# Splitting the shared weights w13 once in the up stages, storing both parts, and grouping rank-2 products by twos

## What is computed

```python
# first: I = 2752; of |silu| the lower-ranked half of each row is set to 0
s = silu(x @ w_gate.T); s[k = I/2 smallest |s| per row] = 0
x1 = layernorm(x + (s * (x @ w_up.T)) @ w_down.T)
# second: weights tiled four times along the input, and rank-2 terms
lin(x, wq, A, B) = x @ tile(wq, (1, 4)).T + 0.5 * (x @ A.T @ B.T)
out = layernorm(x1 + lin(silu(lin(x1, w1q, a1, b1)) * lin(x1, w3q, a3, b3), w2q, a2, b2))
```

## Time and profile before

| | us |
|---|---|
| median of 3 runs | 1863.69 (1860.75 to 1864.17) |
| the profiled execution | 1862.13 |
| its span | 1860.2 |
| TensorE busy (products) | 1840.7 |
| VectorE, ScalarE, GpSimd busy | 1468.3, 719.9, 957.5 |
| DMA, mean over the span | 139 GB/s |

### The profile page before, as it was taken

How to read it: one execution, slowest core, us unless ns; L and a number is a source line. 1 busy time by engine, 2 the same in 40 slices (tenths; PEclk the granted TensorE clock), 3 DMA queues, 4 the chain that set the end, 5 groups by cost and what they waited for, 6 DMA issues and landing times.

```text
span 1860.2 us, 23661 instructions
## 1 busy us (share of the span) xinstructions
PE 1840.7 (99%) x8584; PEld 1533.3 (82%) x8584; DVE 1468.3 (79%) x2077; ACT 719.9 (39%) x1177; POOL 957.5 (51%) x705
## 2 busy tenths in 40 slices
PE   9999999999999999999999999999999999999998
PEld 8898888978889789888888988888887777777776
DVE  2138899988988695898878768988588899889973
ACT  4346544474233434722343365233323232223312
POOL 5446697546655854465466545554568232023410
PEclk9999999999999999999999999999999999999999
DMA  4333248734377743334786334366953112312212
GB/s 147 93 101 97 86 147 236 204 98 142 97 232 227 226 129 104 113 128 131 236 256 195 93 107 142 98 212 193 278 179 141 35 46 101 135 62 77 102 46 91
DMA packets 123511, 258.65 MB, mean 139 GB/s; under 512 B 13860, under 2 KB 35876, under 8 KB 120168
## 3 DMA queue, kind: packets, MB, share of 16 engines
q1 hardware_dynamic: 118784, 240.34, 41.7%
q10 hardware_dynamic: 4608, 16.78, 2.2%
HBM read 215.65 MB, written 41.42 MB: 138 GB/s over the span
## 4 chain that ended last, share of the span: by engine, by line
PE 83%; POOL 5%; DVE 5%; ACT 4%; DMA 3%; issue 1%; SPq 0%; POOLq 0%; DVEq 0%; ACTq 0%
PE banks L1596 28%; PE banks L1597 27%; PE banks L1598 27%; POOL wl L659 3%; ACT junka L815 2%; DMA w_in_place<-in_wg 2%; DVE junkx L1083 1%; PE banks L1788 1%; POOL xTl L659 1%; ACT wh L766 1%; POOL w2l L659 1%; DMA w_in_place<-in_wd 0%; DVE qa L1125 0%; POOL w L688 0%; PE banks L1801 0%
## 5 line engine op out<-in xcount | busy, mean ns | idle before, releaser
L659 POOL TENSOR_TENSOR wl<-w_in_place,wh 128x512 fp32r<-128x512 f32 (+2 forms) x552 | 751.8, 1367 | 573.1 <-ACT wh L766 571.9
L766 ACT CAST wh<-w_in_place 128x512 fp32r<-128x512 f32 (+2 forms) x560 | 329.0, 589 | 724.2 <-DMA w_in_place<-in_wg 281.2
L1596 PE MATMUL banks<-wh,xTh 128*128 128x512 f32 (+2 forms) x1536 | 565.0, 368 | 5.4 <-POOL wl L659 5.3
L1598 PE MATMUL banks<-wh,xTl 128*128 128x512 f32 (+2 forms) x1536 | 563.2, 367 | 0.0
L1597 PE MATMUL banks<-wl,xTh 128*128 128x512 f32 (+2 forms) x1536 | 563.1, 367 | 0.0
L1596 PEld LDWEIGHTS banks<-wh,xTh 128*128 128x128 f32 x1536 | 288.3, 188 | 51.4 <-POOL wl L659 9.6
L1598 PEld LDWEIGHTS banks<-wh,xTl 128*128 128x128 f32 x1536 | 288.3, 188 | 40.1
L1597 PEld LDWEIGHTS banks<-wl,xTh 128*128 128x128 f32 x1536 | 288.3, 188 | 39.6
L1596 PE MATMUL banks<-wh,hTh 128*128 128x512 f32 x672 | 263.2, 392 | 2.2 <-POOL wl L659 2.1
L1598 PE MATMUL banks<-wh,hTl 128*128 128x512 f32 x672 | 262.2, 390 | 0.0
L1597 PE MATMUL banks<-wl,hTh 128*128 128x512 f32 x672 | 262.2, 390 | 0.0
(11 more groups left out here) (151 smaller groups left out, 2194.9 us busy)
## 6 DMA issues: line engine op xcount, KB each, us to landing
w_in_place<-in_wd SPq DMA_DIRECT2D x176, 256.0 KB, 2.7
w_in_place<-in_wg SPq DMA_DIRECT2D x128, 256.0 KB, 3.0
w_in_place<-in_wu SPq DMA_DIRECT2D x128, 256.0 KB, 2.7
turning<-squares SPq DMA_DIRECT2D x16, 1024.0 KB, 5.1
landed<-turning SPq DMA_DIRECT2D x64, 256.0 KB, 3.9
w_in_place<-in_w SPq DMA_DIRECT2D x54, 256.0 KB, 2.9
x_in_place<-in_xT SPq DMA_DIRECT2D x32, 256.0 KB, 5.2
y<-in_xtok SPq DMA_DIRECT2D x4, 2048.0 KB, 8.5
```

Source lines behind the costliest of these rows:

```text
L659: nc.gpsimd.tensor_tensor(lo, landed, hi.bitcast(F32), ALU.subtract).then_inc(done, 1)
L766: nc.scalar.copy(hi, piece).then_inc(hi_done, 1)
L1596: nc.tensor.matmul(dst, ah, bh, start=start, stop=False)
L1598: return nc.tensor.matmul(dst, al, bh, start=False, stop=stop)
```

## The change

- In up of block b = 1 to 3, w13 is split piece by piece, a piece being one of the 22 (pair, w) tiles of 128 x 512. Piece q is loaded by SyncE at i = 14 + 4k (k the count within the block, at most 8), cast by ScalarE and subtracted by GpSimd behind their own work of i + 2, and both parts are stored to a new DRAM tensor `split13` by SyncE at i + 4, where SyncE waits for `w13_lo`. Blocks 1 and 2 take eight pieces (i = 14 to 42), block 3 six (to 34). The buffers are the places of `xt`.
- In both halves `load_13` loads both parts, four transfers of 256 KB a pair; `high_13` and `low_13` are gone. The first two pairs are loaded at d = 40 and 42 of the last down. `w13h` and `acc` change places.
- In pairs 1 to 10, bb = 1 issues its rank-2 products first, right behind those of bb = 0, with both `s_done` and `h_done` waited for in front of them; its dense products follow, the last one of each w signalling.

```diff
+SPLIT_AT, SPLITS = 14, 8
+def splits(b):
+    return [(q, SPLIT_AT + 4 * (q - SPLITS * (b - 1))) for q in range(2 * PAIRS) if q // SPLITS == b - 1]
...
+                        for q, at_piece in splits(b):
+                            if i == at_piece:
+                                load_split(b, q)
+                        for q, at_piece in splits(b):
+                            if i == at_piece + 4:
+                                keep_split(q)
                     if b < NB - 1 and i >= NG - 3:
                         load_x(b + 1, i - (NG - 3))
+            def load_split(b, q):
+                if q % SPLITS == 0:
+                    sp.wait_ge(u_freed, 8 + 4 * NJ * b + 1)
+                    sp.sem_inc(passed_sp, 1)
+                if q >= 2:
+                    sp.wait_ge(w13_out, 32 * (q - 1))
+                sp.sem_inc(passed_sp, 1)
+                sp.dma_start(raw13[q % 2][:, :], w13[q // 2, q % 2, :, :]).then_inc(raw13_in[q % 2], 16)
+            def keep_split(q):
+                sp.wait_ge(w13_lo, q + 1)
+                sp.sem_inc(passed_sp, 1)
+                sp.dma_start(split13[q // 2, q % 2, 0], hi13[q % 2][:, :].bitcast(F32)).then_inc(w13_out, 16)
+                sp.dma_start(split13[q // 2, q % 2, 1], lo13[q % 2][:, :].bitcast(F32)).then_inc(w13_out, 16)
...
             def load_13(h, p):
                 n = PAIRS * h + p
                 if n >= 2:
-                    sp.wait_ge(w13_used, n - 1)
+                    sp.wait_ge(uu_done, 4 * (n - 1))
...
-                    sp.dma_start(w13_in_place[:, n % 2, w, :], w13[p, w, :, :]).then_inc(w13_in[n % 2][w], 16)
+                    sp.dma_start(w13h[:, n % 2, w, :].bitcast(F32), split13[p, w, 0]).then_inc(w13_in[n % 2][w], 16)
+                    sp.dma_start(w13l[:, n % 2, w, :].bitcast(F32), split13[p, w, 1]).then_inc(w13_in[n % 2][w], 16)
...
+            def low_split(q):
+                pool.wait_ge(w13_hi, q + 1)
+                less(hi13[q % 2][:, :], lo13[q % 2][:, :], raw13[q % 2][:, :], w13_lo)
...
+            def high_split(q):
+                act.wait_ge(raw13_in[q % 2], 16 * (q // 2 + 1))
+                nc.scalar.copy(hi13[q % 2][:, :], raw13[q % 2][:, :]).then_inc(w13_hi, 1)
...
+            def low_rank_terms(h, p, bb, first):
+                s, rows = number(h, p, bb), rows_of(p // 2)
+                for i in range(2):
...
+                    for w, done in enumerate((gg_done, uu_done)):
+                        p0 = QUAD[2 * i + w]
+                        ins = nc.tensor.matmul(banks[4 * (s % 2) + 2 * w + i][0:rows, :], b13[p0:p0 + 3 * R, mm],
+                                               lx[p0:p0 + 3 * R, bb, :], start=first, stop=not first)
+                        if not first:
+                            ins.then_inc(done, 1)
...
+                first = p > 0 and bb == 1
+                if first:
+                    pe.wait_ge(s_done, s - 1)
+                    pe.wait_ge(h_done, s - 1)
+                    pe.sem_inc(passed_pe, 1)
+                    low_rank_terms(h, p, bb, True)
...
                     if bb == 0:
-                        pe.wait_ge(w13_lo, 2 * n + w + 1)
+                        pe.wait_ge(w13_in[n % 2][w], 32 * (n // 2 + 1))
...
-                                        k == 0, False)
+                                        k == 0 and not first, first and k == KQ - 1)
+                        if first:
+                            ins.then_inc((gg_done, uu_done)[w], 1)
...
+                if not first:
+                    low_rank_terms(h, p, bb, False)
```

More of the change, by code:

```diff
@@ L93 @@
 FOLDS = 2 * CQ
+SPLIT_AT, SPLITS = 14, 8
+assert SPLIT_AT + 4 * SPLITS < NG and (NB - 1) * SPLITS >= 2 * PAIRS
 SENT_0 = (16, 20, 24, 32, 36, 43)
@@ L204, in program @@
     folded = nc.dram_tensor("folded", (3, P, NT * HQ), F32, kind="Internal").ap()
+    split13 = nc.dram_tensor("split13", (PAIRS, 2, 2, P, 512), F32, kind="Internal").ap()
     turning = nc.dram_tensor("turning", (NB, NJ, P, NT * CW), F32, kind="Internal").ap()
@@ L279, in program @@
         assert at["scr"] + 5 * H <= at["mags"]
+        places = (at["scr"], at["junkd"])
+        hi13 = [sb(f"hi13{i}", [P, 512], F32R, 4, offset=o) for i, o in enumerate(places)]
+        lo13 = [sb(f"lo13{i}", [P, 512], F32R, 4, offset=o + 2048) for i, o in enumerate(places)]
+        raw13 = [sb(f"raw13{i}", [P, 512], F32, 4, offset=o + 2048) for i, o in enumerate(places)]
         over = {"at": at["v"]}
@@ L308, in program @@
         lx = put("lx", [P, 2, TB], F32R)
-        acc = put("acc", [P, 2, R, TB], F32)
+        w13h = put("w13h", [P, 2, 2, 512], F32R)
         assert over["at"] <= at["y"]
@@ L318, in program @@
         hq1l = put("hq1l", [P, CQ, TB], F32R)
-        w13h = put("w13h", [P, 2, 2, 512], F32R)
+        acc = put("acc", [P, 2, R, TB], F32)
         assert over["at"] <= at["sgn"]
@@ L323, in program @@
         fold = (sb("fold0", [P, CQ, TB], F32, 4, offset=at["hq0l"]), sb("fold1", [P, CQ, TB], F32, 4, offset=at["hq1l"]))
-        w13_in_place = sb("w13_in_place", [P, 2, 2, 512], F32, 4, offset=at["w13l"])
         ya = (sb("ya0", [P, 2, H], F32, 4, offset=at["w13l"]), sb("ya1", [P, 2, H], F32, 4, offset=at["w13h"]))
@@ L377, in program @@
             sem("small_in"), sem("b_zero"), sem("b_in"), sem("b_ready"), sem("sel_ready"))
-        w13_hi, w13_lo, w13_used = sem("w13_hi"), sem("w13_lo"), sem("w13_used")
+        raw13_in, w13_out = [sem(f"raw13_in{i}") for i in range(2)], sem("w13_out")
+        w13_hi, w13_lo = sem("w13_hi"), sem("w13_lo")
         l_ready = sem("l_ready")
@@ L470, in load_tokens @@
                 sp.wait_ge(x1_out, 16 * NT * (b + 1))
+                if t == 0:
+                    sp.sem_inc(passed_sp, 1)
+                    sp.wait_ge(w13_out, 32 * min(SPLITS * (b + 1), 2 * PAIRS))
                 if n >= 2:
@@ L583, in load_13 @@
                     sp.sem_inc(passed_sp, 1)
-                    sp.dma_start(w13_in_place[:, n % 2, w, :], w13[p, w, :, :]).then_inc(w13_in[n % 2][w], 16)
+                    sp.dma_start(w13h[:, n % 2, w, :].bitcast(F32), split13[p, w, 0]).then_inc(w13_in[n % 2][w], 16)
+                    sp.dma_start(w13l[:, n % 2, w, :].bitcast(F32), split13[p, w, 1]).then_inc(w13_in[n % 2][w], 16)
             def load_y(b):
                 if b % 2 == 0:
-                    sp.wait_ge(w13_used, PAIRS * (b // 2 + 1))
+                    sp.wait_ge(uu_done, 4 * PAIRS * (b // 2 + 1))
                     sp.sem_inc(passed_sp, 1)
@@ L621, in _ @@
                     x_tiles(NB - 1)
-            for p in range(2):
-                load_13(0, p)
+                if d in (40, 42):
+                    load_13(0, (d - 40) // 2)
             for h in range(2):
@@ L713, in _ @@
                     low_gu(up_at(b), i)
+                    for q, at_piece in splits(b):
+                        if i == at_piece + 2:
+                            low_split(q)
                     if i == KH - 1:
@@ L723, in _ @@
                     less(w2h[0:rows, c, sl], w2l[0:rows, c, sl], w2_in_place[0:rows, c, sl], w2_lo)
[L725 to L729, removed]
             def low_q(h, c, bb):
@@ L838, in up @@
                         turned(b, KH * j + i)
+                        for q, at_piece in splits(b):
+                            if KH * j + i == at_piece + 2:
+                                high_split(q)
                         if j == 2:
                             norm(b - 1, i)
+            def high_split(q):
+                act.wait_ge(raw13_in[q % 2], 16 * (q // 2 + 1))
+                nc.scalar.copy(hi13[q % 2][:, :], raw13[q % 2][:, :]).then_inc(w13_hi, 1)
             def norm(b, i):
@@ L936, in _ @@
                     nc.scalar.copy(w2h[0:rows, c, sl], w2_in_place[0:rows, c, sl]).then_inc(w2_hi, 1)
[L939 to L945, removed]
             def high_xf(b, k):
@@ L1731, in turn_folded @@
                 ins.then_inc(xf_turned, 1)
+            def low_rank_terms(h, p, bb, first):
+                s, rows = number(h, p, bb), rows_of(p // 2)
+                for i in range(2):
+                    mm = slice((2 * p + i) * P, (2 * p + i) * P + rows) if p < PAIRS - 1 else \
+                        slice(2 * p * P + i * rows, 2 * p * P + (i + 1) * rows)
+                    for w, done in enumerate((gg_done, uu_done)):
[4 more added lines that the diff above has]
+                            ins.then_inc(done, 1)
             def pair(h, p, bb):
@@ L1755, in pair @@
                     if bb == 0:
-                        pe.wait_ge(w13_lo, 2 * n + w + 1)
+                        pe.wait_ge(w13_in[n % 2][w], 32 * (n // 2 + 1))
                         pe.sem_inc(passed_pe, 1)
-                    if p:
+                    if p and not first:
                         pe.wait_ge((s_done, h_done)[w], s - 1)
```

11 lines of the change are left out of this document (1 added, 10 removed).

## The result

The changed kernel takes **1881.11 us** (median of 4 runs, 1879.31 to 1881.5); the kernel before, run beside it, 1862.44. The ratio is 1.010, with a 95% interval of 1.0087 to 1.0113: **slower by 1.0%**, where 1862.8 was forecast. The profiled execution took 1881.5 us, 19.4 more than that of before.

A forecast was written before the change was run, and what follows sets the result against it. TensorE's own instruction stream, busy 1840.7 of 1860.2 us, was taken as the bound. Grouping -8.0, start of the second network -0.9 and ends of up +8.0 sum to -0.9 us: forecast 1862.8 us, range 1856.5 to 1870.

The forecast's parts named there:

- The grouping: Rank-2 products of pairs 1 to 10: a merged place costs 0.86 us instead of 1.26, 8.0 us saved in 20 places.
- Rival 3: Merged rank-2 groups cost nearly two single ones: saving only 0 to 3 us, time 1869; chance 0.06.
- The cover of the earlier wait: Wait for h_done moves 2.8 us forward in the halves; costed at nothing, since VectorE catches up; 10 us if uncovered.
- rival 4: TensorE's earlier wait for VectorE at the merged groups binds: 20 x 0.25 = 5 us, time 1868; chance 0.04.
- under 0.85 us in the mean: Sign on VectorE: its accumulation takes less than this, against 0.900 us in the mean before.
- The start of the second network: TensorE no longer waits 1.00 us for GpSimd's w13l there: 0.9 us saved, bounds 0 and 1.0.
- The split in up: Among 512-wide pieces, SyncE waits about 0.8 us and issues two stores within TensorE's 2.7 us a piece: cost 0.
- The ends of up 1 and up 2: Stores delay piece 47 and the first gate piece: 3.5 us lost in block 1, 4.5 in block 2, 8.0 in all.
- Rival 1: The ends of up swallow the delay: loss 0 to 5 us, time 1858; chance 0.31.
- Block 3 at 0: Up of block 3 stores its last piece at i = 38, still 384 wide and before the end: no loss.
- Rival 2: SyncE's queue becomes the bound in up, i = 38 to 47 of blocks 1 and 2: 8 us each, 1870; chance 0.18.
- Its second price: After a long TensorE stall, eight dense steps take 3.36 us and not 1.84: 1.5 us more, under rival 2.

The follow-up runs named there:

- e4: The changed kernel without the grouping, rank-2 products behind the dense ones in every step as before: 1891.75 us, ratio 1.0159.
- e1: The kernel before with only the rank-2 products grouped by twos, w13 still split in the halves: 1860.55 us, ratio 0.9995.
- e9: The changed kernel plus six unused GpSimd subtractions of 128 x 192 per pair in the halves: 1893.56 us, ratio 1.0166.
- e3: The changed kernel with each split piece's load, cast, subtraction and stores cut to 8 of 128 partitions, order and waits kept: 1862.29 us, ratio 0.9999.
- e5: The changed kernel with pieces started at i = 13 + 4k and stored by SyncE six places behind the load, not four: 1859.13 us, ratio 0.9983.
- e2: The changed kernel with each piece's two stores issued by ScalarE behind its work of i + 4, not by SyncE: 1854.78 us, ratio 0.9963.
- e6: The changed kernel with full load, cast and subtraction, but only 8 of 128 partitions of each part stored: 1864.97 us, ratio 1.0018.
- e7: The changed kernel with stores issued by ScalarE and 7, 7, 8 pieces in blocks 1 to 3, not 8, 8, 6: 1852.89 us, ratio 0.9949.

## Why the prediction was wrong

**The grouping: right, to the tenth.** Forecast 8.0 us with 0.86 for a merged place. The timeline of TensorE in the changed kernel:

```profile
1521.60 0.39 PE L1632 MATMUL banks<-xsh,w13l 128*128 128x512 f32 x1
1521.92 0.74 PE L1775 MATMUL banks<-lx,b 6*128 6x512 f32 x8
1522.59 0.50 PE L1630 MATMUL banks<-xsh,w13h 128*128 128x512 f32 x1
1522.92 0.39 PE L1631 MATMUL banks<-xsl,w13h 128*128 128x512 f32 x1
```

From 1521.60 to 1522.92 are 1.32 us with two dense steps (0.46) in them: 0.86, as taken. Over all groups the same count gives 27.7 us before and 19.7 after: 8.0 saved. The second network wins a little more, 9.3 us beside its start (e4 has the start alone, -0.6), or 0.46 for a place; the other 1.3 us lie in the dense products farther behind a group, the first ten of which start up to 0.007 us farther apart than the rest, and where the pairs end. Rival 3 is refuted. The rule of the Trainium skill, "TensorEngine Tiling (Array Packing)", Key Properties, that a second tile of the same mode needs no emptying, agrees: the second four, side by side, cost 0.86 - 0.63 = 0.23, one dense step, as taken.

**The cover of the earlier wait: right, with its condition.** The prediction costed the wait for h at nothing because GpSimd's splits leave, and named rival 4 as what happens otherwise. In the changed kernel no wait of TensorE stands in front of the rank-2 products; in e1 and e9, where GpSimd works beside them, TensorE is idle there for up to 1.3 and 1.5 us. e9 shows the cause: only GpSimd's work was added. The prediction had two prices for the wait uncovered, 10 us in its working and 5 in rival 4; with its clock falls it took 11.3 in e9. The forecast of "under 0.85 us in the mean" for the accumulation is met:

```profile
L1519 DVE SCALAR_TENSOR_TENSOR acc<-h,a2raw,acc 128x512 f32<-128x512 f32 (+1 forms) x168 | 131.4, 822 | 1.5
```

**The start of the second network:** 0.9 forecast, 0.6 found.

**The split in up: the step that failed.** Two sentences of it. The first: SyncE waits "about 0.8 us" in front of its stores, all within TensorE's 2.7 a piece. It waited 3.9 in the mean. The term that was mis-sized is the 2.7 us for the landing of piece i + 2, behind which the split stands on ScalarE and GpSimd. By the landing of each load in the traces, those of the 22 pieces i + 2 took 5.3 us in the mean in the changed kernel. They took 3.7 already before: 2.7 is the median of all 128 loads, and not that of these places. The timeline of SyncE, ScalarE and GpSimd in the changed kernel shows one such place:

```profile
533.96 0.33 SPq L446 DMA_DIRECT2D w_in_place<-in_wu  x1
534.40 0.61 SPq L546 DMA_DIRECT2D raw<-in_w  x1
538.62 0.33 SPq L552 DMA_DIRECT2D split<-hi  x1
539.00 0.43 SPq L553 DMA_DIRECT2D split<-lo  x1
539.53 0.91 SPq L446 DMA_DIRECT2D w_in_place<-in_wu  x1
```

```profile
532.47 0.62 ACT L804 CAST wh<-w_in_place 128x512 fp32r<-128x512 f32 x1 [4.59 <-DMA w_in_place<-in_wu]
```

```profile
535.54 1.29 POOL L699 TENSOR_TENSOR wl<-w_in_place,wh 128x512 fp32r<-128x512 f32 x1 [0.63 <-ACT wh L804]
536.79 1.75 POOL L699 TENSOR_TENSOR lo<-raw,hi 128x512 fp32r<-128x512 f32 x1
```

ScalarE has already stood 4.59 us for a ring piece when it casts at 532.47. The piece in front of the split, i = 20, was issued at 528.51, and landed late; the same load in e3, issued at 529.56, did not. The DMA issues of these two moments:

```profile
w_in_place<-in_wu SPq DMA_DIRECT2D x1, 256.0 KB, 6.3
```

```profile
w_in_place<-in_wu SPq DMA_DIRECT2D x1, 256.0 KB, 3.6
```

In the changed kernel GpSimd's `lo` is over at 538.54, 10.0 us after that load and not 6.3, and nearly all of the difference is the landing, 6.3 and not 2.7. SyncE, through with the load of raw at 535.0, goes on at 538.62: 3.6 us in which no ring load is issued. In e3 `lo` is over 7.3 us after the load, and SyncE waits 1.2. TensorE, at 2.7 us a piece, feels nothing yet (20.00 of 20 us busy, above), since the ring is ahead.

The second: the stores' bytes are small against the ring's slack. By themselves they are (e5, e2: 4.4 and 3.8 us in all), and so is the wait by itself (e3: 9.6, e6: 10.6). **Both together are 29.5, more than twice the sum, 3.8 + 9.6 = 13.4.**

What the runs support is this. The traffic makes the loads land late, whoever waits: the ring loads from i = 18 to the last store take 5.0 us in the mean in the changed kernel and 4.6 to 4.8 in e5, e2 and e7, against 3.7 to 3.8 with small stores (e6, e3) and 3.3 before. Where SyncE has to wait for what stands behind such a load, the late landing makes its wait long, 3.9 us in the mean and not 2.4 (e3) or 2.3 (e6), and the ring loads behind the wait are then issued late and land late as well (192 KB in 4.9 us; 2.7 with small stores, 3.1 to 3.6 with full stores and no such wait). The ring's slack swallows one of the two and not both, once the pieces are narrow and TensorE takes 12 x 0.17 = 2.0 and then 12 x 0.15 = 1.8 us a piece. An estimate from these rows: four pieces of 2.0 are 8 us ahead. At i = 38 of up 1 the changed kernel waits 6.4 us (577.66 to 584.03), and with a landing of 4.9 that is 11.3; e3 waits 1.2 there, with 2.7 it is 3.9; e5 has a landing of 3.1 alone.

At the end of up 1 the timeline of SyncE is then:

```profile
598.21 0.37 SPq L446 DMA_DIRECT2D w_in_place<-in_wu  x1
605.27 0.33 SPq L552 DMA_DIRECT2D split<-hi  x1
605.64 0.43 SPq L553 DMA_DIRECT2D split<-lo  x1
606.18 0.39 SPq L455 DMA_DIRECT2D x_in_place<-in_xT  x1
606.68 0.39 SPq L446 DMA_DIRECT2D w_in_place<-in_wu  x1
607.17 0.39 SPq L465 DMA_DIRECT2D turning<-squares  x1
607.67 0.37 SPq L455 DMA_DIRECT2D x_in_place<-in_xT  x1
608.15 0.96 SPq L446 DMA_DIRECT2D w_in_place<-in_wg  x1
```

The order is the one that the prediction wrote down (two stores, x, piece 47, squares, x, gate), and it is held up 6.7 us (598.58 to 605.27) and not 3.4; the first gate piece goes at 608.15 and not at 597.9 as forecast, against 595.04 before.

**The ends of up 1 and up 2: right in kind and size, as far as they stand alone.** 8.0 forecast; e3, with the order and few of the bytes, loses 9.6 there. Rival 1, that the ends swallow the delay, is refuted by it.

**Block 3 at 0: wrong.** It lost 6.5 us, bit by bit from i = 22 on. With small pieces (e3) or without the wait (e2, e5) it loses 0.0, 0.0 and 0.1. With small stores and full loads (e6) it is 2.2, from i = 40 on, so the load of the piece may have a part in it beside the stores.

**Rival 2** named SyncE's queue in up as the bound, and it was, with 12.1 and 10.9 us in blocks 1 and 2 instead of 8 each. Its price, 1870, was too small. SyncE's waits for the squares grew as this rival said, from 18.8 us in 13 places to 35.6 in 14, so 1.1 us each (1 to 2 forecast). A longer store is not the reason: the 1 MB store of the squares lands in 5.2 us in the median, 5.1 before. The Trainium skill, "DMA: Bandwidth & Descriptors", on the anatomy of one DMA, has a transfer's own semaphore wait for the write receipt, and tells it for transfers that GpSimd issues; that 44 stores in front would lengthen another transfer by it was the prediction's reading, and no run bears it out. The waits may have grown since SyncE comes to them without having waited for TensorE first; no run shows that by itself. Its second price is there: the first products of gate 3 in the changed kernel, after an idle time:

```profile
982.26 0.50 PE L1630 MATMUL banks<-wh,xTh 128*128 128x512 f32 x1 [2.30 <-POOL wl L699]
982.57 0.62 PE L1631 MATMUL banks<-wl,xTh 128*128 128x512 f32 x1
982.99 0.63 PE L1632 MATMUL banks<-wh,xTl 128*128 128x512 f32 x1
...
985.55 0.59 PE L1632 MATMUL banks<-wh,xTl 128*128 128x512 f32 x1
```

From 982.26 to 985.55 eight steps take 3.29 us and not 1.84, after 2.30 us of idle: 1.45 more; the granted clock is 1.00 from 978 to 982 and 0.54 from 982.26 to 985.80, so the 1.2 GHz level for nearly all of it. This comes behind the 22.7 us by which the stage starts late; since the kernel before has one such place too, and the changed kernel hasn't that one, it is no part of the difference.

**The sum, term by term:** grouping with the start of the second network -8.9 forecast, -9.9 measured; ends of up +8.0, +9.6 by e3; what the prediction set at 0, 29.5 - 9.6 = +19.9; the other stages -0.3. Together +19.3 where -0.9 was forecast.

**What stays open.** Whether the loads land late because they stand behind the stores in the queues or because stores to HBM take bandwidth from them. In the changed kernel, where SyncE issues the stores first and then all loads that it owes, the two stores land in 2.6 and 3.2 us in the median and the 192 KB loads in 4.9; in e5 the stores take 5.0 and 5.7 and the loads 3.1. So the order has a part; how large it is, no run tells. Nor does a run give SyncE a wait of a chosen length, which would show where the ring's slack ends; the 8 us above are an estimate. How e5's 3.3 us in up 2 and some 2 us after it come about was not traced. Why VectorE's accumulation is slower in the changed kernel (822 ns) than in e4 (757), with the same work of GpSimd, was not looked into.

## What to carry to other kernels

A store whose operand is made by another engine holds up every load behind it in the same queue until the operand is there: put it where its operand has been ready for a while, or let an engine that is not feeding the ring issue it, and do not price its wait with the median landing of all loads from the trace of before: read the landing at the places in question, and expect the change's own traffic to lengthen it. Waits and traffic in one queue are not two terms of a sum: most of each alone vanished in the slack here, and together they cost more than twice the sum. When a wait moves forward, ask which engine must be early for it and what slows that engine; here the grouping and the freed GpSimd brought nothing one by one (+0.5 and -0.6 us) and 9.9 us in the second network together.

## What the runs showed of the hardware

The same accumulation on VectorE, 168 times 128 x 512, takes in the mean 757 ns (e4) and 822 (the changed kernel) without GpSimd's splits in the halves, 900 (before) and 923 (e1) with 65 us of them, and 969 (e9) with 95 us of other GpSimd work: 28% from end to end, and no row of waits tells of it. TensorE stayed at 20.00 of 20 us busy with the DMA engines at a share of 1.02 and 355 GB/s (e5, 530 to 550), its loads issued in time. Four rank-2 products between dense ones cost 0.63 us, eight in one place 0.86. Behind idle times of TensorE of 1.80 us (before), 2.30 (the changed kernel) and 1.13 (e1) the granted clock fell to 0.50 for some eight products. And the same load of 192 KB took 2.5 us in the median before, 2.7 with small stores (e3, e6), 3.1 to 3.6 with full stores and no wait for the low part in front of it (e5, e7, e2), and 4.9 in the changed kernel.
